# One decoder kernel: row statistics of a pair taken one stage earlier, and a wait on additions split by PSUM bank

## The reference

```
x = x + softmax_attention(layernorm(x))
#   q = softmax(h @ Wq.T + bq, features); k = softmax(h @ Wk.T + bk, tokens) / 16
#   v = softmax(h @ Wv.T + bv, tokens);   out = (q @ k.T) @ v
x = x + retention(layernorm(x), ctx)
x = x + moe_swiglu(layernorm(x))
x = x + lie_rotation(layernorm(x))
x = x + one_key_attention(layernorm(x), ctx)      # softmax attention, 16 heads, one shared key and value head
x = x + moe_silu(layernorm(x))
#   shared = silu(h @ sW1 + sb1) @ sW2 + sb2
#   act = sqrt(softplus(h @ routing_W.T + expert_bias)); the 2 largest of 8 weigh their experts
#   layernorm(h) = (h - mean) / sqrt(var + 1e-5), over the 256 features, no weights
```

## Time and profile before

| | |
|---|---|
| median of 3 runs (lowest, highest) | 1630.08 us (1628.37, 1632.9) |
| profiled execution, time | 1620.8 us |
| its span | 1619.1 us |
| mean granted TensorE clock | 0.836 |
| busy: PE, DVE, ACT, POOL | 1265.6, 1073.6, 820.3, 656.4 us (78, 66, 51, 41% of the span) |
| chain that ended last, by line | L3225 5%, L3211 5%, L3297 1%, then below 1% each |

### The profile page before, as it was taken

The page is one execution under the profiler, slowest core; times in us unless marked ns, Lnnn a source line. Parts: engine busy times, 40 slices in busy tenths (PEclk is TensorE's granted clock), DMA queues, the critical chain, the costliest instruction groups (busy, mean ns, idle before and its releaser), DMA issues. The chain is left out here.

```text
span 1619.1 us, 33536 instructions
## 1 busy us (share of the span) xinstructions
PE 1265.6 (78%) x12367; PEld 967.2 (60%) x12367; DVE 1073.6 (66%) x2063; ACT 820.3 (51%) x1529; POOL 656.4 (41%) x595
## 2 busy tenths in 40 slices
PE   5888578789763359999999648874778775799997
PEld 2555356667652349999999538632555553556664
DVE  5878578887754556666666383666788784576553
ACT  4767457666533324444444222133577767566643
POOL 1222148887852025555555210061478776000000
PEclk9989788888766569999999955556899975899999
DMA  7665376546507212222322180003533320241240
GB/s 273 223 206 206 115 139 107 99 96 94 73 2 299 119 53 93 93 91 91 115 80 76 40 329 1 2 1 74 130 72 67 61 35 7 100 132 49 87 128 27
DMA packets 100057, 165.26 MB, mean 102 GB/s; under 512 B 14902, under 2 KB 63802, under 8 KB 98620
## 3 DMA queue, kind: packets, MB, share of 16 engines
q1 hardware_dynamic: 90876, 138.20, 30.8%
q0 software_dynamic: 8640, 24.65, 4.8%
q10 hardware_dynamic: 384, 0.26, 0.1%
HBM read 110.61 MB, written 52.30 MB: 101 GB/s over the span
## 5 line engine op out<-in xcount | busy, mean ns | idle before, releaser
L3006 POOL TENSOR_TENSOR q_pl<-q_ex,q_ph 128x512 f16<-128x512 f32 x128 | 147.8, 1164 | 57.3 <-ACT q_ph L2945 55.8
L1781 POOL TENSOR_TENSOR r_siml<-r_sim,r_simh 128x512 f16<-128x512 f32 x128 | 155.8, 1239 | 33.4 <-ACT r_simh L1692 33.2
L1087 POOL DMA_INDIRECT expert_results<-mt_yout,m_deliver x78 | 77.4, 992 | 148.9 <-ACT mt_yout L1175 136.8
L1692 ACT ACTIVATE r_simh<-r_sim 128x512 f16<-128x512 f32 x128 | 79.9, 627 | 87.3 <-DVE r_sim L1555 80.5
L1120 PE MATMUL mt_pU<-mt_xh,m_w 128*128 128x256 f16 x624 | 116.1, 274 | 1.5 <-DVE mt_xl L1205 1.5
L2671 DVE TENSOR_REDUCE q_mx<-q_pS 128x4 f32<-128x512 f32 x128 | 87.0, 682 | 45.0 <-PE q_pS L2565 44.1
L1120 PE MATMUL mt_pV<-mt_xh,m_w 128*128 128x256 f16 x624 | 115.2, 273 | 0.0
L1079 POOL DMA_INDIRECT mt_xin<-token_rows,m_fetch x78 | 86.7, 1112 | 68.2 <-POOLq L778 44.7
L1555 DVE TENSOR_TENSOR r_sim<-r_pS,r_causal 128x512 f32<-128x512 f32 x128 | 86.8, 682 | 34.1 <-PE r_pS L1467 33.8
L1169 ACT ACTIVATE mt_hh<-ahead 128x512 f16<-128x512 f32 x78 | 49.2, 631 | 117.9 <-DVE ahead L1214 117.9
L2939 ACT ACTIVATE q_ex<-q_pE 128x512 f32<-128x512 f32 x128 | 76.4, 598 | 63.7 <-PE q_pE L2586 48.8
(11 more groups left out here) (579 smaller groups left out, 4037.2 us busy)
## 6 DMA issues: line engine op xcount, KB each, us to landing
s_spread_share<-shares SPq DMA_DIRECT2D x32, 512.0 KB, 6.8
a_pf<-in_L_ffn_W SPq DMA_DIRECT2D x24, 512.0 KB, 6.7
m_w<-split_w SPq DMA_DIRECT2D x6, 2048.0 KB, 22.0
split_w<-a_ph SPq DMA_DIRECT2D x24, 256.0 KB, 3.8
split_w<-a_pl SPq DMA_DIRECT2D x24, 256.0 KB, 4.3
r_kstack<-k_bounce SPq DMA_DIRECT2D x48, 128.0 KB, 4.1
r_qstack<-q_bounce SPq DMA_DIRECT2D x48, 128.0 KB, 5.3
q_Q<-m_bounce SPq DMA_DIRECT2D x24, 256.0 KB, 6.7
```

The costliest lines, as they stand in the source:

```text
L1087: pool.indirect_dma_start(results[:, :], bass.IndirectOffsetOnAxis(ap=deliver[:, at:at + 1], axis=0), yout[n % 2][:, a, :], None).then_inc ...
L1692: act.activation(simh[n % RING][:, :], sim[n % SIMS][:, :], ACT.Copy).then_inc(s["simh"], 1)
L1781: pool.tensor_tensor(siml[n % RING][:, :], sim[n % SIMS][:, :], simh[n % RING][:, :], ALU.subtract)\
L3006: pool.tensor_tensor(pl[n % RING][:, :], ex[n % 3][:, :], ph[n % RING][:, :], ALU.subtract)\
```

## The change

There are two edits. In the first stage `project_q` no longer waits for the four additions of the group before at once: before its first batch it waits for two of them, and before its third for all four. Between the fifth and the sixth stage, the bn_stats and the combination of the second pair (batches 8 to 15) move: the vector engine issues them in the last group of the fifth stage, two bn_stats in each of the units 8 to 11 and the seven small operations in unit 12, behind that unit's `finish`. The mean and the variance are kept in two tiles that both stages know (`X0["mean"]`, `X0["ve"]`). In the sixth stage `stats` and `combine` are left out for this pair, GpSimd's `invert(1)` waits for nothing, and the counts that later pairs wait for are lower by one pair. `negate(1)` stays where it was.

```diff
@@ -407,10 +407,10 @@
                 def project_q(g):
                     if g == 0:
                         pe.wait_ge(s["bias_low"], 1)
-                    else:
-                        pe.wait_ge(s["x_done"], GB * g)
                     steps = [(dc, x, y) for dc in range(DC) for x, y in TERMS]
                     for b in range(GB):
+                        if g > 0 and b % 2 == 0:
+                            pe.wait_ge(s["x_done"], GB * (g - 1) + b + 2)
                         out = rows(pB)[:, b, :]
                         pe.matmul(out, ones[:, :], bias_rows[:, :], start=True, stop=False)
                         for n, (dc, x, y) in enumerate(steps):
@@ -2405,6 +2405,9 @@
         e_stat = c.sb("e_stat", [P, PAIR, 6])
         e_apart, e_apart2, e_both, e_dev, e_devs, e_mean, e_ve, e_rstd, e_top, e_best, e_top2, e_best2 = (
             c.sb("e_" + n, [P, PAIR]) for n in "apart apart2 both dev devs mean ve rstd top best top2 best2".split())
+        f_stat = c.sb("f_stat", [P, PAIR, 6])
+        f_apart, f_apart2, f_both, f_dev, f_devs = (c.sb("f_" + n, [P, PAIR]) for n in "apart apart2 both dev devs".split())
+        f = {n: c.sem("f_" + n) for n in "stat summed scaled ve".split()}
         e_rows = [c.sb(f"e_rows{i}", [P, GB, D]) for i in range(2)]
         (e_lg, e_ab, e_ex, e_u, e_um, e_ln, e_lnt, e_quo, e_l1p, e_l1px, e_pos, e_sp, e_act, e_picked, e_val, e_first, e_masked,
          e_second, e_chosen) = (c.sb("e_" + n, [P, PAIR, E]) for n in (
@@ -2857,6 +2860,26 @@
                                       e_chosen[:, :, :].rearrange("p (a b) e -> p a b e", a=2), ALU.mult)\
                        .then_inc(e["share"], 1)
 
+                def stats_second(b):
+                    if b == 0:
+                        dve.wait_ge(s["x_done"], 2 * PAIR)
+                    dve.bn_stats(f_stat[:, b, :], X[:, PAIR + b, :]).then_inc(f["stat"], 1)
+
+                def combine_second():
+                    mean_e, dev_e, mean_o, dev_o = (f_stat[:, :, n] for n in (1, 2, 4, 5))
+                    dve.wait_ge(f["stat"], PAIR)
+                    dve.tensor_tensor(f_apart[:, :], mean_e, mean_o, ALU.subtract).then_inc(f["summed"], 1)
+                    dve.tensor_tensor(f_both[:, :], mean_e, mean_o, ALU.add).then_inc(f["summed"], 1)
+                    dve.tensor_tensor(f_dev[:, :], dev_e, dev_o, ALU.add).then_inc(f["summed"], 1)
+                    dve.wait_ge(f["summed"], 3)
+                    dve.tensor_tensor(f_apart2[:, :], f_apart[:, :], f_apart[:, :], ALU.mult).then_inc(f["scaled"], 1)
+                    dve.tensor_scalar(X0["mean"][:, :], f_both[:, :], 0.5, None, ALU.mult).then_inc(f["scaled"], 1)
+                    dve.tensor_scalar(f_devs[:, :], f_dev[:, :], 1.0 / D, LN_EPS, ALU.mult, ALU.add)\
+                       .then_inc(f["scaled"], 1)
+                    dve.wait_ge(f["scaled"], 3)
+                    dve.scalar_tensor_tensor(X0["ve"][:, :], f_apart2[:, :], 0.25, f_devs[:, :], ALU.mult, ALU.add)\
+                       .then_inc(f["ve"], 1)
+
                 def early(u):
                     if u < 4:
                         stats_early(2 * u)
@@ -2882,6 +2905,11 @@
                         choose_first_early()
                     if u == 6:
                         choose_second_early()
+                    if 8 <= u <= 11:
+                        stats_second(2 * u - 16)
+                        stats_second(2 * u - 15)
+                    if u == 12:
+                        combine_second()
 
                 for t in KM:
                     dve.memset(t[:, :], 0.0).then_inc(s["made"], 1)
@@ -3157,8 +3185,9 @@
             def _(pool):
                 def invert(q):
                     at = slice(q * PAIR, (q + 1) * PAIR)
-                    pool.wait_ge(s["ve"], q)
-                    pool.tensor_tensor(rstd[:, at], ve[:, at], power[:, 0:PAIR], ALU.pow).then_inc(s["rstd"], 1)
+                    if q > 1:
+                        pool.wait_ge(s["ve"], q - 1)
+                    pool.tensor_tensor(rstd[:, at], ve[:, at] if q > 1 else X0["ve"][:, :], power[:, 0:PAIR], ALU.pow).then_inc(s["rstd"], 1)
 
                 pool.memset(parts[:, :, :], 0.0).then_inc(s["filled"], 1)
                 pool.wait_ge(s["filled"], 1)
@@ -3339,23 +3368,23 @@
                 def combine(q):
                     at = slice(q * PAIR, (q + 1) * PAIR)
                     mean_e, dev_e, mean_o, dev_o = (stat[:, at, n] for n in (1, 2, 4, 5))
-                    dve.wait_ge(s["stat"], q * PAIR)
+                    dve.wait_ge(s["stat"], (q - 1) * PAIR)
                     dve.tensor_tensor(apart[:, at], mean_e, mean_o, ALU.subtract).then_inc(s["summed"], 1)
                     dve.tensor_tensor(both[:, at], mean_e, mean_o, ALU.add).then_inc(s["summed"], 1)
                     dve.tensor_tensor(dev[:, at], dev_e, dev_o, ALU.add).then_inc(s["summed"], 1)
-                    dve.wait_ge(s["summed"], q * 3)
+                    dve.wait_ge(s["summed"], (q - 1) * 3)
                     dve.tensor_tensor(apart2[:, at], apart[:, at], apart[:, at], ALU.mult).then_inc(s["scaled"], 1)
                     dve.tensor_scalar(mean[:, at], both[:, at], 0.5, None, ALU.mult).then_inc(s["scaled"], 1)
                     dve.tensor_scalar(devs[:, at], dev[:, at], 1.0 / D, LN_EPS, ALU.mult, ALU.add)\
                        .then_inc(s["scaled"], 1)
-                    dve.wait_ge(s["scaled"], q * 3)
+                    dve.wait_ge(s["scaled"], (q - 1) * 3)
                     dve.scalar_tensor_tensor(ve[:, at], apart2[:, at], 0.25, devs[:, at], ALU.mult, ALU.add)\
                        .then_inc(s["ve"], 1)
 
                 def negate(q):
                     at = slice(q * PAIR, (q + 1) * PAIR)
                     dve.wait_ge(s["rstd"], q)
-                    dve.scalar_tensor_tensor(shift[:, at], mean[:, at], -1.0, rstd[:, at], ALU.mult, ALU.mult)\
+                    dve.scalar_tensor_tensor(shift[:, at], mean[:, at] if q > 1 else X0["mean"][:, :], -1.0, rstd[:, at], ALU.mult, ALU.mult)\
                        .then_inc(s["shifted"], 1)
 
                 def rows_low(g):
@@ -3472,7 +3501,7 @@
                                     (-10, take_logits), (-9, add_one), (-8, softplus), (-7, choose_first),
                                     (-6, choose_second), (-5, cut)):
                         q = routed(k, at)
-                        if q is not None:
+                        if q is not None and (q > 1 or at > -20):
                             run(q)
                     if k == -6:
                         split.low(dve, [0, 1])
@@ -3543,7 +3572,8 @@
             if name == "mqa":
                 first = Core(nc, whole, [], "first_")
                 A["first_pair"] = {"XH": first.sb("XH", [P, DC, 2 * GT], f16), "XL": first.sb("XL", [P, DC, 2 * GT], f16),
-                                   "share": first.sb("share", [P, 2, E, GB])}
+                                   "share": first.sb("share", [P, 2, E, GB]),
+                                   **{n: first.sb(n, [P, 2 * GB]) for n in ("mean", "ve")}}
             work[name](nc, sems, X, ident, power, A, ahead)
             give_back(nc, sems)
             sems = []
```

## The result

Against 1631.2 us for the kernel before (median of four runs, 1628.4 to 1632.9), the changed kernel took **1619.2 us** (four runs, 1615.8 to 1620.1). The ratio is 0.9927 [0.9914, 0.9941], so 11.9 us less, with an interval from 9.6 to 14.0. The forecast was 8.3 less, 1621.8 in a range from 1615 to 1628. Direction and range held; the gain was under-forecast by 3.6 us.

A forecast was written before the change was run, and what follows sets the result against it. Bounds: TensorE's 8.10 us wait for normalized rows at the last boundary and its 13.6 us of waits for additions in stage one. Terms -5.3 - 3.0 + 0 = -8.3 us, from 1630.1 to 1621.8; 8 in 10 from 1615 to 1628.

The forecast's parts named there:

- Part one: Last stage boundary: with the second pair's statistics gone, the shift is ready earlier and TensorE's gap shrinks; -5.3 us.
- more is won: Rival, 0.17: clock stays up at the boundary and fourth loop, or GpSimd does not hold scalings; about -11.5, 1618.5 us.
- Part two: Last group of one-key attention: moved statistics fit into the vector engine's idle time; 0, range up to 0.7 us.
- Part three: Stage one: queries start after two additions, 0.78 us earlier, gaining in four loops; -3.0 us, bounds 0 and -6.7.
- the 1.2 us for the clock: Stage one, fourth loop: if its low clock goes, 1.2 us on top of the 0.78; not in the sum.
- the three loops held before: Stage one's second, third and sixth loops: scaling ends with GpSimd's subtraction, so an earlier maximum wins nothing.
- the rival in which GpSimd does not hold: Stage one: scalings not held by GpSimd, -2.5 us more; one case of "more is won" (0.17).
- both clock terms of that rival: In "more is won" (0.17): clock stays up at the last boundary, -1.65, and in stage one's fourth loop, -1.2.
- Only one part pays: Rival, 0.15: vector engine meets a new wait in stage one, leaving the last boundary's 5.3; 1624.8 or 1627.2 us.
- slower: Rival, 0.06: retention stage starts earlier and its low clock stretches fall elsewhere, 12.8 us more; 1634.6 us.

The follow-up runs named there:

- the repeat of before: The kernel before, unchanged, run again for a second trace: 1635.1 us, ratio 1.0.
- the statistics alone: Kernel before with only the second pair's statistics moved, queries waiting for all four additions: 1621.6 us, 0.9935; again 1625.5 us, 0.9954.
- the scaling variant: Changed kernel with the scaling of the queries' maximum moved from the vector engine to ScalarE: 1619.3 us, 0.9902.
- bank by bank alone: Kernel before with only the queries' wait for the additions split by bank: 1628.1 us, 0.9987; again 1630.4 us, 0.9979.
- experiment 6: Not a number: "the experiment" is the changed kernel with scaling on ScalarE, expected "6 to 7 us" shorter in stage one; 1619.3 us, 0.9902.
- the best kernel: Changed kernel with scaling on ScalarE, plus last stage's negation and four normalized rows issued earlier: 1613.5 us, 0.9879; again 1613.0 us, 0.9888.
- the scaling variant of the kernel before: Kernel before with the scaling of the queries' maximum moved to ScalarE: 1635.8 us, 1.0002.

## Why the prediction was right, and where its size was off

**Part one, -5.3 forecast, -6.9 measured in the first pair of traces.** The mis-sized term is the one that was set to zero: "I take neither, as 2.8 lies between the two gaps." The step itself went as described: power behind the memsets, shift behind the bias row, TensorE's gap 2.17 us where 2.8 was forecast. But the clock was at 1.00 behind the gap, and the low stretch of 3.3 us went too, priced at 1.65. 5.3 and 1.65 are 6.95. The traces tell the two terms apart. From the start of the stage, the transposes come at 13.33 us in all five traces with the moved statistics and the old order behind them, and at 18.72 or 18.73 in all six without: 5.4. What follows the transposes took 226.2 to 226.6 us against 227.7 to 229.1: 1.1 to 2.9 for the clock, the most where it stayed low longest (0.73 over the next 10 us in the repeat of before, 0.84 in its first trace). The last stage took 239.5 to 240.0 us in the five traces of the changed kernel, of the statistics alone and of the scaling variant, and 246.4 to 247.8 in the six traces whose last stage computes its own statistics. In those five the transposes took 1.09 us, behind gaps from 1.63 to 2.85 us; in the six they took 1.97, behind gaps from 7.02 to 8.20. Half of the rival "more is won" came true here.

**Part two, 0 forecast, 0 measured.** The bn_stats ran unhindered, 2.71 us for eight. Of the seven small operations four were stretched, to 0.65, 1.13, 1.07 and 1.14 us, and three took 0.16. All were done at 1365.6, before the reciprocal of 1366.16. The last four reciprocals are 14.55 us apart from first to last, 14.51 before. The kernel with the work added and unused says 0 by its time.

**Part three, -3.0 forecast, -3.0 measured in the loops of the first pair of traces, -4.4 as a mean of all.** The end of each scaling carries the loop on. Loop by loop, in the first pair of traces, it came earlier, relative to the loop before, by 0, 0, 0, 0.64, 0.85, 0, 0.79 and 0.77 us (the ends are at 35.92, 54.77, 73.61, 95.91, 116.21, 135.66, 153.19 and 170.71 us before and at 35.96, 54.81, 73.67, 95.33, 114.78, 134.25, 150.99 and 167.74 after). The forecast had 0.78, 0.68, 0.78 and 0.78 for the fourth, fifth, seventh and eighth.

That the sum is just the forecast is in part luck. From the first scaling's end to the eighth's, the five traces without the split and with the scaling on the vector engine take 134.8 to 135.5 us; the changed kernel's first trace takes 131.8, but the three others with the split (its repeat, and bank by bank alone twice) take 130.3 to 130.4. The fourth loop makes the difference: there it won 0.64 us in the first trace and 2.0 to 2.1 in the other three, where the clock behind its gap of 2.30 or 2.31 us was 0.76 over 7 us and not 0.53. That is the 1.2 us for the clock that the prediction named and left out of its sum. The 0.8 us that stage one gained behind the last loop in the first pair (3.8 in all) is not the edit's: from the eighth scaling to the end of the stage it takes 13.7 to 14.7 us without the split, 13.6 to 16.1 with it. Over all, stage one ends at 185.2 us as a mean of five without it and at 181.3 of four with it: 3.9.

Four scalings took 1.57 to 1.58 us, as expected, and the two kernels with the scaling on ScalarE show that the hold is a cause: there the maxima of the second and third loop lie 18.18 us apart without the split and 17.39 with it, against 18.85 and 18.85.

By the rule of the Trainium skill that the prediction cited (page "SBUF — State Buffer", section "Who interferes with whom"; the shared ports as an exclusive lock) the three loops held before gain nothing, and the trace agrees, with 0 us won in the second, third and sixth loop and 1.57 to 1.58 us for a scaling of 0.17.

What was mis-sized is the rival in which GpSimd does not hold. It had 2.5 us more, and the expectation of the experiment 6 to 7 us of stage one. From the first maximum to the eighth the split with a free scaling won 9.95 us (132.91 to 122.96), and with a held one 3.0 in the first pair and 4.4 as the mean. In three of its seven loops it won 2.26 to 2.28 us, 0.78 from the split and 1.5 from the clock, which fell in all three without the split and in none with it; in the best kernel's traces it fell in one of the three again, and 8.5 us were won. The hold swallows the clock's part too: in the changed kernel's fifth loop the gap was 1.41 us instead of 2.19, the clock stayed up, the maximum came 2.25 us earlier relative to the loop before, and the scaling then waited for GpSimd and kept 0.85 of it.

**The sum.** The first pair of traces gives -3.8 for stage one, -6.9 for the last stage and 0 for the tail, so -10.7; the repeats of both kernels give -3.2 and -8.0, so -11.2; the means over all traces give -3.9 and -7.3, again -11.2. The times have 11.9 and 11.6, with an interval of 9.6 to 14.0 for the first. So the two stages carry nearly all of the gain, and the 3.6 us beyond the forecast of 8.3 are the clock at the last boundary, 1.65, the clock in stage one, about 1, and a rest of about 1 that the scatter covers. By the size of the gain the result stands nearer to the rival "more is won" (about -11.5) than to the forecast, and it has both clock terms of that rival (the one in stage one in three traces of four), though not the free scalings.

The one-key attention stage may hold some gain too. From its first statistics to the last reciprocal it took 267.1 to 269.8 us in the seven traces with the moved statistics, and 269.0 to 273.8 in the five without; with the added work alone it had 268.7. The difference builds up over the whole stage and not in its last group, and the two sets touch. Why is open. The one trace with the added work alone lies with the faster set, so what is added to this stage's program may matter more than what it is used for; its time, 0.8 us less with an interval that holds 0, doesn't settle it.

**The rest.** "Only one part pays" and "slower" fell: both halves show in their own stages, and retention and dispatch kept 404 to 406 us in the changed kernel. Carrying the difference over to the median was right; where the 9.3 us between the profiled run and the median lay was not asked, and the runs showed it: nearly all in the expert tiles, beside all terms.

## What to carry to other kernels

When a gap of TensorE is cut, ask from rows what the clock does behind the gap that is left; here that was 1.1 to 2.9 us on top of the gap's own 5.4. When a wait is moved and the next small operation of the vector engine shares a time with a GpSimd operation, look whether it just grows by what was won; with that one operation of 0.17 us on ScalarE the split was worth 8.6 to 9.8 us of stage one in the traces instead of 3.9, and moving it was worth nothing measurable without the split. And compare two traces stage by stage, with more than one trace of each kernel and all from one chip: a stage that nobody touched differed by 13.6 us between two executions of one kernel, more than the whole change, and by about 4 us between chips; and a forecast that one pair of traces met to 0.1 us was 1.4 off the mean of nine.

## What the runs showed of the hardware that was not expected

- The clock behind a gap did not go by the gap's length. In the last stage it stayed at full behind gaps of 1.63 to 2.85 us. In front of the fourth loop of stage one, a gap of 2.06 us left it at 1.00 in the scaling variant of the changed kernel, and gaps of 2.06 and 2.07 us lost it in the best kernel's two traces (0.76 over the next 7 us). The kernel before kept it behind 3.09 us in its repeat and lost it behind 3.08 in its first trace; in front of the second loop it was the other way round, lost behind 1.59 us in the repeat and kept behind 1.58 in the first. The rows of the repeat, fourth loop and second:

```profile
88.75:95.75 7.00, 7.00 (x46) 4.31 (x47) 5.05 (x14) 3.09 (x13) 4.95 (x3) 1.00 0.34 133
48.85:55.85 7.00, 7.00 (x36) 3.75 (x37) 3.56 (x14) 2.22 (x9) 4.95 (x3) 0.76 0.49 193
```

  Nor does TensorE's work before the gap tell them apart: in front of the fourth loop it had been busy for 7.01 of 7.70 us at a granted clock of 1.00 in each of these traces, whether the clock then fell or not. Before the gap in the last stage, behind which it stayed up, it was 6.25 of 6.30 us at 0.64. What decides is not seen in these rows, so for a gap of this size the clock's part is a chance and belongs into the range.
- A 128x4 scaling with one operand is held by GpSimd's 128x1024 subtraction, to 1.58 us from 0.17, as two-operand ones were beside GpSimd's 128x512 subtractions, to 1.07 to 1.14 us from 0.16; GpSimd's 128x1024 subtraction took a median of 2.13 us with held scalings (the changed kernel) and without (the scaling variant of the kernel before).
- One kernel's expert tiles, fed by indirect DMAs, took 314.1 us in one execution and 327.7 in another, at a granted clock of 0.99 in both. TensorE waited there for the vector engine's low halves (`mt_hl`) for 10.0 us in the slow one, for 5.7 in the changed kernel (322.8 us), and not at all in the fast one.
